# Two attention stages over a 12544-row context: another place for GpSimd's low parts, the chunk transfers, the row statistics and the decay factors

## The reference

```python
# L0: 16 heads of 64, 128 queries, 12544 keys
k, v = jnp.split(context @ w_kv, 2, axis=-1)
attn = softmax(einsum('bhid,bhjd->bhij', x @ w_q, k) * scale)
out = einsum('bhij,bhjd->bhid', attn, v)
# L1: 8 heads of 64; the context is normalised first, and a mask and 128 more keys come in
layernorm(x, g, b) = (x - mu) * rsqrt(var + EPS) * g + b
# next block of L0, prepared here: a power of the decay for each distance
weights = decay ** jnp.maximum(diff - 1.0, 0.0) * causal
```

## Time and profile before

| | |
|---|---|
| time, median of 3 runs | 2619.31 us (2619.17 to 2630.63) |
| the profiled execution's own time | 2626.45 us |
| its span, first to last instruction | 2624.7 us |
| mean granted clock of TensorE | 0.937 |
| PE busy | 2335.8 us (89%) |
| DVE busy | 2007.8 us (76%) |
| ACT busy | 1266.9 us (48%) |
| POOL busy | 730.4 us (28%) |
| stage l0x, from its first matmul to its last value product | 5.56 to 1173.4 us |
| stage l1x, likewise | 1338.1 to 1885.8 us |

### The profile page before, as it was taken

The page is one execution under the profiler, slowest core; times in us unless marked ns, Lnnn a source line. Parts: engine busy times, 40 slices in busy tenths (PEclk is TensorE's granted clock), DMA queues, the critical chain, the costliest instruction groups (busy, mean ns, idle before and its releaser), DMA issues. The chain is left out here.

```text
span 2624.7 us, 61865 instructions
## 1 busy us (share of the span) xinstructions
PE 2335.8 (89%) x23416; PEld 1876.9 (72%) x23416; DVE 2007.8 (76%) x4001; ACT 1266.9 (48%) x2509; POOL 730.4 (28%) x907
## 2 busy tenths in 40 slices
PE   8997999999999999977868989999667579999986
PEld 7886888888888888866757777777443247888873
DVE  7989899999999999975867888878652367666615
ACT  5544555555555555434645555555311264555553
POOL 1433143432443423330134545554000010010000
PEclk9999999999999999987989999999777689999996
DMA  6566556666666666556637777776377653444310
GB/s 258 204 225 220 211 204 235 238 238 241 220 217 225 239 239 227 201 186 224 218 120 267 265 263 262 259 257 241 134 306 289 252 183 118 128 142 128 88 48 23
DMA packets 179170, 540.96 MB, mean 206 GB/s; under 512 B 18012, under 2 KB 113456, under 8 KB 172736
## 3 DMA queue, kind: packets, MB, share of 16 engines
q1 hardware_dynamic: 176352, 528.52, 56.6%
q0 software_dynamic: 2304, 8.39, 0.9%
q10 hardware_dynamic: 224, 0.10, 0.0%
HBM read 356.76 MB, written 180.19 MB: 205 GB/s over the span
## 5 line engine op out<-in xcount | busy, mean ns | idle before, releaser
L511 PE MATMUL l0x_psum<-l0x_fast 128*128 128x512 f32 x1764 | 435.8, 399 | 1.5 <-DVE l0x_fast L713 1.0
L756 DVE STREAM_TRANSPOSE l0x_sbuf<-l0x_sbuf 128x896 f32<-128x896 f32 x224 | 388.9, 1778 | 0.6 <-issue 0.6
L511 PEld LDWEIGHTS l0x_psum<-l0x_fast 128*128 128x128 f32 x1764 | 323.1, 188 | 90.1 <-issue 22.6
L625 ACT ACTIVATE l0x_sbuf<-l0x_sbuf 128x896 f32<-128x896 f32 x224 | 234.7, 1048 | 281.3 <-DVE l0x_sbuf L736 281.3
L1808 DVE CUSTOM_DVE_ANT_0 l3x_sbuf<-l3x_psum,key_bias,l3x_sbuf 128x896 f32<-128x896 f32 x224 | 249.2, 1151 | 92.6 <-PE l3x_psum L1652 76.8
L1738 ACT ACTIVATE l3x_sbuf<-l3x_psum 128x512 f32<-128x512 f32 x392 | 221.4, 599 | 179.0 <-PE l3x_psum L1670 172.4
L491 PE MATMUL l0x_psum<-l0x_fast 128*128 128x448 f32 x1344 | 300.2, 372 | 0.0
L491 PEld LDWEIGHTS l0x_psum<-l0x_fast 128*128 128x128 f32 x1344 | 244.2, 188 | 25.0 <-DVE l0x_fast L719 0.3
L736 DVE CUSTOM_DVE_ANT_0 l0x_sbuf<-l0x_psum,l0x_sbuf 128x896 f32<-128x896 f32 x224 | 248.8, 1149 | 10.1 <-PE l0x_psum L526 10.1
L552 PE MATMUL l0x_psum<-l0x_sbuf 128*32 128x128 f32 x6272 | 204.6, 280 | 36.3 <-DVE l0x_sbuf L775 27.7
L552 PEld LDWEIGHTS l0x_psum<-l0x_sbuf 128*32 128x32 f32 x6272 | 173.5, 111 | 72.6 <-issue 61.2
(11 more groups left out here) (778 smaller groups left out, 4348.6 us busy)
## 6 DMA issues: line engine op xcount, KB each, us to landing
turns<-l0x_sbuf SPq DMA_DIRECT2D x112, 896.0 KB, 3.7
l0x_sbuf<-turns SPq DMA_DIRECT2D x112, 896.0 KB, 4.9
turns<-l1x_sbuf SPq DMA_DIRECT2D x56, 896.0 KB, 4.2
l1x_sbuf<-turns SPq DMA_DIRECT2D x56, 896.0 KB, 5.7
last_keys<-ctx_high SPq DMA_DIRECT2D x112, 224.0 KB, 3.5
ahead<-in_L_ffn_W SPq DMA_DIRECT2D x18, 1024.0 KB, 11.4
experts<-in_L_ffn_W SPq DMA_DIRECT2D x18, 1024.0 KB, 12.4
l0x_sbuf<-in_ctxT SPq DMA_DIRECT2D x14, 896.0 KB, 5.0
```

The source lines that it names most:

```text
L511: mm = pe.matmul(ps[:, :], x[:, c, t * T:(t + 1) * T], weights[w][:, c, :], start=(j == 0), stop=(j == len(products) - 1))
L625: act.activation(p, p, ACT.Exp, scale=-1.0, bias=self.negm[:, n % 2, 2 * pr + a:2 * pr + a + 1], accum_out=self.rs[:, m % self.RING, a:a + ...
L756: dve.transpose(self.blocks[:, j, :, a * CT:(a + 1) * CT, :].rearrange("p g t c -> p t g c"), self.p[:, a, :].rearrange("p (t r g) -> p t ...
```

## The change

The arithmetic is the same; the instructions stand elsewhere.

- SP issues the gather ahead of the chunk's transfers, no longer behind them. In l1x mean and rstd are sent apart: rstd at pr = 0, mean at pr = 3 for chunk n + 3 (for chunk 2 at n = 0, pr = 0), each with its own wait. In l0x the rows of the next chunk are sent at pr = 6 instead of at its pr = 0.
- ACT computes alpha of m in step m, no longer in step m + 1.
- POOL does the low parts and the bias ahead of the row sums of step pr = 0, and `pool_norm` at pr = 1 instead of pr = 2, operation by operation over both halves instead of half by half.
- DVE in l0x takes the tiles' row statistics at pr = 0 (two), 1, 2, 3 (one each) and 6 (two), instead of one in each of pr = 1 to 7. The decay's bits stand at n = 2, pr = 0 to 3, and n = 3, pr = 0 to 2.

`norm_part` is split into `norm_center`, `norm_scale` and `norm_gain`; where l1x normalises chunk 0 on DVE, the three are called in the old order (that part of the diff is left out).

```diff
@@ -375,8 +375,8 @@
         for m in range(self.P * NCH):
             n, pr = divmod(m, self.P)
             self.sp_scatter(sp, m)
+            self.sp_gather(sp, m)
             self.chunk_transfer(sp, n, pr)
-            self.sp_gather(sp, m)
             if m == 0 and self.side is None:
                 self.sp_out(sp)
             if m == self.P * NCH - 1 and self.side is not None:
@@ -386,20 +386,22 @@
     def chunk_transfer(self, eng, n, pr):
 
         s, ahead = self.s, n + 2
-        if pr == 0 and n > 0 and self.side is not None:
-            self.side.sp_rows(eng, n)
-        if pr == 0 and ahead < NCH and self.norm_dram is not None:
-            for c in range(DC):
-                eng.wait_ge(s.sem(f"scaled{c}"), ahead)
-            self.sp_norm(eng, ahead)
+        if self.norm_dram is not None and pr == 0 and ahead < NCH:
+            if n == 0:
+                self.sp_mean(eng, ahead)
+            self.sp_rstd(eng, ahead)
         if pr == 1 and ahead < NCH:
             eng.wait_ge(s.sem("c_low"), 2 * ahead)
             self.sp_raw(eng, ahead)
+        if pr in (2, 3) and ahead <= NCH and self.parts_dram is not None:
+            self.sp_save(eng, n + 1, pr - 2)
         if pr == 2 and ahead < NCH and self.mask_dram is not None:
             eng.wait_ge(s.sem("bias"), ahead)
             self.sp_mask(eng, ahead)
-        if pr in (2, 3) and ahead <= NCH and self.parts_dram is not None:
-            self.sp_save(eng, n + 1, pr - 2)
+        if pr == 3 and ahead + 1 < NCH and self.norm_dram is not None:
+            self.sp_mean(eng, ahead + 1)
+        if pr == 6 and n + 1 < NCH and self.side is not None:
+            self.side.sp_rows(eng, n + 1)
 
     def sp_scatter(self, sp, m):
 
@@ -423,7 +425,8 @@
         if n < NCH:
             self.sp_raw(sp, n)
             if self.norm_dram is not None:
-                self.sp_norm(sp, n)
+                self.sp_mean(sp, n)
+                self.sp_rstd(sp, n)
         if self.mask_dram is not None and n < NCH:
             sp.wait_ge(s.sem("bias"), n)
             self.sp_mask(sp, n)
@@ -437,9 +440,15 @@
     def sp_raw(self, sp, n):
         sp.dma_start(self.raw[:, :, :], self.keysT_dram[:, :, n * CH:(n + 1) * CH]).then_inc(self.s.sem("raw_in"), 16)
 
-    def sp_norm(self, sp, n):
-        for name, dst, src in (("mean", self.mean, self.norm_dram[0]), ("rstd", self.rstd, self.norm_dram[1])):
-            sp.dma_start(dst[:, :], src[n * CH:(n + 1) * CH].partition_broadcast(128)).then_inc(self.s.sem(name + "_in"), 16)
+    def sp_mean(self, sp, n):
+        for c in range(DC):
+            sp.wait_ge(self.s.sem(f"centered{c}"), n)
+        sp.dma_start(self.mean[:, :], self.norm_dram[0][n * CH:(n + 1) * CH].partition_broadcast(128)).then_inc(self.s.sem("mean_in"), 16)
+
+    def sp_rstd(self, sp, n):
+        for c in range(DC):
+            sp.wait_ge(self.s.sem(f"scaled{c}"), n)
+        sp.dma_start(self.rstd[:, :], self.norm_dram[1][n * CH:(n + 1) * CH].partition_broadcast(128)).then_inc(self.s.sem("rstd_in"), 16)
 
     def sp_out(self, sp):
         sp.dma_start(self.wo[:, :, :], self.A[self.prefix + "wo"]).then_inc(self.s.sem("wo_in"), 16)
@@ -676,8 +685,8 @@
                 self.act_out(act, m - 2)
             for use in self.plan.get(m, []):
                 self.act_group(act, use)
-            if 0 < m <= self.M:
-                self.act_alpha(act, m - 1)
+            if m < self.M:
+                self.act_alpha(act, m)
             if pr == 0 and n + 1 < NCH:
                 self.act_context(act, n + 1)
 
@@ -812,22 +821,31 @@
             mine = slice(8 * g, 8 * g + 8)
             dve.tensor_tensor(self.acc[:, mine, :], self.acc[:, mine, :], add_cols(self.l[:, mine], self.HD), ALU.mult).then_inc(s.sem("attended"), 1)
 
-    def norm_part(self, eng, n, c):
-        s = self.s
+    def norm_center(self, eng, n, c):
+        s, part = self.s, self.raw[:, c, :]
         eng.wait_ge(s.sem("raw_in"), (n + 1) * 16)
         eng.wait_ge(s.sem("mean_in"), (n + 1) * 16)
+        eng.tensor_tensor(part, part, self.mean[:, :], ALU.subtract).then_inc(s.sem(f"centered{c}"), 1)
+
+    def norm_scale(self, eng, n, c):
+        s, part = self.s, self.raw[:, c, :]
         eng.wait_ge(s.sem("rstd_in"), (n + 1) * 16)
-        eng.wait_ge(s.sem("gain_in"), 32)
-        part = self.raw[:, c, :]
-        eng.tensor_tensor(part, part, self.mean[:, :], ALU.subtract).then_inc(s.sem(f"centered{c}"), 1)
         eng.wait_ge(s.sem(f"centered{c}"), n + 1)
         eng.tensor_tensor(part, part, self.rstd[:, :], ALU.mult).then_inc(s.sem(f"scaled{c}"), 1)
+
+    def norm_gain(self, eng, n, c):
+        s, part = self.s, self.raw[:, c, :]
+        eng.wait_ge(s.sem("gain_in"), 32)
         eng.wait_ge(s.sem(f"scaled{c}"), n + 1)
         eng.tensor_scalar(part, part, self.gain[:, 0, c:c + 1], self.gain[:, 1, c:c + 1], ALU.mult, ALU.add).then_inc(s.sem(f"normed{c}"), 1)
 
     def pool_norm(self, pool, n):
         for c in range(DC):
-            self.norm_part(pool, n, c)
+            self.norm_center(pool, n, c)
+        for c in range(DC):
+            self.norm_scale(pool, n, c)
+        for c in range(DC):
+            self.norm_gain(pool, n, c)
 
     def pool_context(self, pool, n):
         s = self.s
@@ -868,18 +886,18 @@
                 self.side.pool_step(pool, n, pr)
             if self.decay is not None:
                 self.decay.pool_step(pool, n, pr)
+            if pr == 0:
+                if n + 1 < NCH:
+                    self.pool_context(pool, n + 1)
+                if n + 1 < self.N and self.mask_dram is not None:
+                    self.pool_bias(pool, n + 1)
             pool.wait_ge(s.sem("alpha"), m + 1)
             pool.tensor_tensor(self.l[:, hs], self.l[:, hs], self.alpha[:, r, :], ALU.mult).then_inc(s.sem("l_scaled"), 1)
             for a in range(2):
                 pool.wait_ge(s.sem(f"p{a}"), m + 1)
             pool.wait_ge(s.sem("l_scaled"), m + 1)
             pool.tensor_tensor(self.l[:, hs], self.l[:, hs], self.rs[:, r, :], ALU.add).then_inc(s.sem("l"), 1)
-            if pr == 0:
-                if n + 1 < NCH:
-                    self.pool_context(pool, n + 1)
-                if n + 1 < self.N and self.mask_dram is not None:
-                    self.pool_bias(pool, n + 1)
-            if pr == 2 and self.norm_dram is not None and n + 2 < NCH:
+            if pr == 1 and self.norm_dram is not None and n + 2 < NCH:
                 self.pool_norm(pool, n + 2)
 
     def pe_outputs(self, pe, ps):
@@ -912,6 +930,7 @@
 
 
     W = 258
+    ROWS = {0: (0, 1), 1: (2,), 2: (3,), 3: (4,), 6: (5, 6)}
 
     def __init__(self, s, A):
         self.s, self.A = s, A
@@ -970,8 +989,8 @@
                 self.dve_moments(dve, n, t)
         if pr == 4:
             self.dve_scales(dve, n)
-        if pr > 0:
-            self.dve_row(dve, n, pr - 1)
+        for t in self.ROWS.get(pr, ()):
+            self.dve_row(dve, n, t)
 
     def dve_moments(self, dve, n, t):
         s = self.s
@@ -1116,6 +1135,7 @@
 
 
     BITS = 7
+    BIT = {(2 + k // 4, k % 4): k for k in range(BITS)}
 
     def __init__(self, s, A):
         self.s, self.A = s, A
@@ -1150,14 +1170,15 @@
             for k in range(1, self.BITS):
                 link(dve.tensor_tensor(dk[:, k:k + 1], dk[:, k - 1:k], dk[:, k - 1:k], ALU.mult))
             dve.tensor_scalar(self.dm1[:, :], dk[:, :], -1.0, None, ALU.add).then_inc(s.sem("decay"), 1)
-        if n == 2 and pr < self.BITS:
+        if (n, pr) in self.BIT:
+            bit = self.BIT[n, pr]
             dve.wait_ge(s.sem("dl_steps"), 1)
-            dve.wait_ge(s.sem("decay"), max(1, 2 * pr))
-            link = linker(dve, s.sem("decay_bits"), 2 * pr)
-            link(dve.tensor_scalar(self.bit[:, :], self.steps[:, :], pr, 1, ALU.logical_shift_right, ALU.bitwise_and))
-            dst = w if pr == 0 else self.fac
-            link(dve.tensor_scalar(dst[:, :], self.bit[:, :], self.dm1[:, pr:pr + 1], 1.0, ALU.mult, ALU.add))
-            if pr > 0:
+            dve.wait_ge(s.sem("decay"), max(1, 2 * bit))
+            link = linker(dve, s.sem("decay_bits"), 2 * bit)
+            link(dve.tensor_scalar(self.bit[:, :], self.steps[:, :], bit, 1, ALU.logical_shift_right, ALU.bitwise_and))
+            dst = w if bit == 0 else self.fac
+            link(dve.tensor_scalar(dst[:, :], self.bit[:, :], self.dm1[:, bit:bit + 1], 1.0, ALU.mult, ALU.add))
+            if bit > 0:
                 dve.tensor_tensor(w[:, :], w[:, :], self.fac[:, :], ALU.mult).then_inc(s.sem("decay"), 2)
             else:
                 dve.sem_inc(s.sem("decay"), 1)
...
```

8 lines of the change are left out of this document (6 added, 2 removed).

## The result

| | before | after |
|---|---|---|
| median, us | 2624.38 (2618.57 to 2630.65, 14 runs) | 2612.80 (2600.43 to 2621.61, 14 runs) |
| profiled execution, its span | 2624.7 | 2605.2 |
| last sum of l0x | 1163.93 | 1144.04 |
| last high part of l1x | 1804.29 | 1784.85 |

The kernel after takes 0.9955 of the time of the kernel before, 95% interval 0.994 to 0.997: 11.6 us less, where 26 were forecast. In the profiled executions it is 19.5 us, and the two marks inside say where: l0x ends 19.9 us earlier, and l1x, for which 24 us were forecast, takes as long as before (640.8 us between the two marks, before 640.4). These marks are of one execution each, and single executions scatter (2600 to 2622 us after).

What follows compares the result with a forecast made beforehand. PE was taken to set the pace of l0x and l1x, with gains only from its waits and slow clock. Terms: l1x -24, l0x -5 + 6 - 3, together -26 us; against the median 2619.31 that gives 2593 us, range 2572 to 2613.

Steps and rivals of the forecast that it cites:

- The gather's wait, -10: l1x: PE's 21.0 us of gather waits fall by 10 (bounds 0 and -18), about 1 us a chunk staying.
- The ring's order: DMA: one ring is served in order, so a gather issued first isn't delayed; of 21.0 us only the next scatter's share stays.
- ACT's wait, -10: l1x: with normalisation at pr = 1 ACT stops waiting for POOL; PE's 13.3 us fall by 10 (bounds 0 and -13).
- The clock, -3: l1x: fewer slow PE stretches behind waits, -3 us (0 to -4).
- Row statistics, +6: l0x: a second tile behind pr = 6 adds 0.53 us in 12 chunks, +6 us (upper bound +8, lower -11).
- rival B: l0x: DVE's difference of pr = 6 slips ahead of POOL's addition, -17 us on the sum, 2576 us; chance 0.15.
- The decay's bits, -5: l0x: bits leave POOL's long side work but meet its low parts at pr = 0; -5 us (+2 to -12).
- l0x's gathers, -3: l0x: of 8.4 us of PE's gather waits, the 4 in mid-stage shrink, -3 us (0 to -4).
- Alpha, 0: ACT: computing alpha a step earlier costs nothing.
- C: l1x: the DMA chain refills the waits, gather's and most of ACT's gains lost; l1x -7, total 2610 us; chance 0.26.
- D: l1x: POOL's moved normalisation holds two of DVE's differences a chunk, +50 us, 2643 us; chance 0.06.

Runs made afterwards that it cites:

- e1: Kernel after, with SP sending the chunk's transfer ahead of the gather again, as before; 2568.36 us, 0.9791 of the kernel before.
- order G: SP's issue order scatter, gather, transfer, as in the kernel after (2612.80 us).
- e11: Kernel after, with l1x's transfers at pr = 0 to 2 issued on ACT's queue, pr = 3's on SP; 2629.16 us, 1.0023 of the kernel before.
- e2: Kernel before, with only SP's gather moved ahead of the chunk's transfer; 2645.82 us, 1.0081 of the kernel before.
- order S: SP's issue order scatter, transfer, gather, as in the kernel before (2624.38 us).
- e6: Kernel after, with SP's order, row statistics, decay bits and alpha put back as before; 2579.29 us, 0.9836 of the kernel before.
- e3: Kernel before, with only l0x's row statistics and the rows' transfer moved; 2618.14 us, 0.9984 of the kernel before.
- e4: Kernel before, with only the decay bits spread over pr = 0 to 3 of chunks 2 and 3; 2615.49 us, 0.9972 of the kernel before.
- e12: Kernel after, with SP's old order, one decay bit a chunk at pr = 7 and alpha one step later; 2551.63 us, 0.9730 of the kernel before.

## Why the prediction was wrong

Forecast 2593 us, measured 2612.8, at the range's upper edge of 2613; the direction was right and the size less than half. That it lies inside the range is luck, since two large misses stood against each other: l1x gave nothing where 24 us were forecast, and l0x gave 19.9 (between marks) where 2 were.

- **The gather's wait, -10: the step that failed.** "The change helps twice ... and the gather goes first." Going first took 1.3 us off the gather and put 3.1 on the next scatter, which the next values wait for. In 410 us the waits rose by 14.6 instead of falling by 10, and with the clock this ate all that the other moves gave; e1, which takes back this one edit, gives 43 us. I had the row (7.1 us where 4 are usual) and named the mechanism in the same paragraph, but priced it at 1 us a chunk, for the raw context alone, as if the steps were independent. In order G each of the four steps has a transfer behind its gather (the masks, which were to cost "nothing", among them), and a late scatter makes the next one late.
- **The ring's order.** I cited the Trainium skill ("DMA: Bandwidth & Descriptors", section "Queues, rings and completion order"): each DMA engine takes up what one ring holds in its order. The gather's fall from 6.2 to 4.9 us agrees. By the same rule the scatter stands behind the transfer; I said so for the raw context only, and let it cost 1 us a chunk. e11 shows that this half isn't the rule's alone: without the shared queue the scatter took 6.2 us, against 4.4 in e1.
- **ACT's wait, -10: right as a mechanism.** In steady l1x L605 no longer waits for POOL, and the turns wait 3.5 us instead of 13.3. But a wait on PE is only worth its time if no other ends behind it. e2 shows this: with nothing moved on POOL and slower gathers, ACT's waits fell to 5.0 us by themselves. Under order S the two moves on POOL gave 39 us between the marks of l1x (e6), where I had 24 for all of it.
- **The clock, -3:** it went the other way, 0.99 to 0.97, behind 21 waits instead of 15; in e1, with waits of at most 1.1 us, it is 1.00.
- **Row statistics, +6: wrong side of an edge that I had named.** The difference arrived 0.02 us ahead of POOL's addition, and rival B happened: -11 us in l0x's marks with the rows alone (e3). "The edge is not passed by the numbers" weighed a margin of 0.04 us, and on such margins the outcome changed from chunk to chunk (held in two of 14 after, in four of 14 in e3); 0.15 was too little for it.
- **The decay's bits, -5:** e4 measured -7 (-12 to -3); the two waits behind pr = 0 were 2.76 and 2.82 us for my 3.0.
- **l0x's gathers, -3:** nothing after (9.5 us of waits, before 8.4). e2's l0x ended 3.0 us earlier (2.0 of it in that first chunk), but e1's ends 5.2 us before that of the kernel after.
- **Alpha, 0:** right under order S, the only one in which it was tried (e12).
- **The rivals.** B held in l0x, where it gives -2 - 17 = -19; the marks say -19.9. C held in l1x with the right cause (gather waits of over 1.5 us a chunk; L605 behind POOL didn't come), but at 0 where I had priced it at -7. I gave each a case of its own and none to both at once. D didn't come: in all of l1x two differences were held for over 1 us, 2.13 and 1.53. In e1 six were, up to 2.07 us, and PE hardly waited.
